# Part of the PSUM evictions moved from VectorE to ScalarE in a transformer layer on eight cores

## What is computed

```python
# attention part (input: layer-normed x)
xa = x @ (W_attn + lora).T                     # 3072 channels: q, k, v
xa = batchnorm(xa)                             # mean and variance over all 8*4096 rows
att = softmax(causal(q @ k.T / 32))
y = (att @ v) @ W_proj.T @ (W_proj + lora).T
x = x + layernorm(y)

# feed-forward part (input: layer-normed x)
aq(x) = round(x * 127 / max|x| per row), wq(w) = round(w / mean|w|) cut to -1..1
gate = silu(aq(x) @ wq(w_gate).T * scales)     # 1024 -> 4096
up   = aq(x) @ wq(w_up).T * scales             # 1024 -> 4096
down = aq(gate * up) @ wq(w_down).T * scales   # 4096 -> 1024
x = x + layernorm(down)
```

## Time and profile before

| | us |
|---|---|
| two timed runs | 6860.9 and 6988.77, median 6924.84 |
| profiled execution | 6855.12 |
| span of its slowest core (core 4) | 6853.6 |
| busy in it: PE, DVE, ACT, POOL | 4191.5, 2681.4, 859.0, 740.4 |
| stage 1b (1820 to 2211) | 391 |
| stage 4a (4665 to 5900) | 1235 |
| stage 4b (6008 to the end) | 846 |

### The profile page before, as it was taken

How to read it: one execution, slowest core, us unless ns; L and a number is a source line. 1 busy time by engine, 2 the same in 40 slices (tenths; PEclk the granted TensorE clock), 3 DMA queues, 4 the chain that set the end, 5 groups by cost and what they waited for, 6 DMA issues and landing times.

```text
span 6853.6 us, 63291 instructions; the slowest of 8 cores (6833.6 to 6853.6 us)
## 1 busy us (share of the span) xinstructions
PE 4191.5 (61%) x19100; PEld 1796.2 (26%) x19100; DVE 2681.4 (39%) x3728; ACT 859.0 (13%) x1490; POOL 740.4 (11%) x2436
## 2 busy tenths in 40 slices
PE   5455555799898124555556641116878787467676
PEld 2111111222443012222222221012333333233333
DVE  2444444300443233333333234445555555632322
ACT  0222222100000001111111111111111111000000
POOL 0244444300000000000000000000000000000000
PEclk9988888899999568788888885557989898688888
DMA  3766665565122211100000014441111111312221
GB/s 131 222 190 193 189 191 190 170 176 149 39 85 83 86 46 39 35 28 31 23 24 16 23 40 147 154 141 59 37 47 37 44 40 37 135 65 83 82 79 71
DMA packets 227896, 626.48 MB, mean 91 GB/s; under 512 B 56376, under 2 KB 81000, under 8 KB 215208
## 3 DMA queue, kind: packets, MB, share of 16 engines
q1 hardware_dynamic: 207080, 555.32, 25.9%
q0 software_dynamic: 20480, 67.13, 2.4%
HBM read 450.39 MB, written 171.97 MB: 91 GB/s over the span
## 4 chain that ended last, share of the span: by engine, by line
PE 48%; DVE 19%; issue 11%; DMA 10%; POOL 9%; ACT 1%; DVEq 1%; POOLq 1%; SPq 0%; ACTq 0%
PE pall L1322 8%; PE pall L1214 6%; PE pall L1207 6%; PE pall L680 5%; PE pall L930 4%; PE pall L532 4%; DVE lnx L491 3%; PE pall L827 2%; PE pall L845 2%; POOL lnx_scr L58 2%; POOL smalls L488 2%; PE pall L950 2%; PE pall L538 2%; PE pall L968 2%; DMA vbn<-xa_scr 1%
## 5 line engine op out<-in xcount | busy, mean ns | idle before, releaser
L508 PE MATMUL pall<-lnx 128*128 128x512 bf16 x2048 | 614.0, 453 | 456.0 <-DVE lnx L491 456.0
L1207 PE MATMUL pall<-WgT,kqT 128*128 128x512 bf16 x2048 | 536.5, 410 | 248.2 <-DVE kqT L1196 248.2
L1322 PE MATMUL pall<-WdT,gqT 128*128 128x512 bf16 x2048 | 516.1, 419 | 31.1 <-DVE gqT L1312 31.1
L1214 PE MATMUL pall<-WuT,kqT 128*128 128x512 bf16 x2048 | 500.8, 389 | 6.0 <-DVE gu L1226 5.9
L508 PEld LDWEIGHTS pall<-lnx 128*128 128x128 bf16 x2048 | 204.9, 108 | 864.8 <-issue 731.9
L491 DVE TENSOR_SCALAR lnx<-xin,smalls 128x1024 bf16<-128x1024 f32 x256 | 208.1, 813 | 565.3 <-POOL smalls L488 565.3
L827 PE MATMUL pall<-Kfm,qfm 128*128 128x512 bf16 (+3 forms) x480 | 167.9, 529 | 372.6 <-DVE smalls L896 341.9
L473 ACT ACTIVATE dummy1k<-xin 128x1024 f32<-128x1024 f32 x256 | 270.8, 1058 | 738.7 <-DMA xin<-x_all 738.2
L680 PE MATMUL pall<-lnfm,WqkvT 128*128 128x512 bf16 x1536 | 347.2, 390 | 6.2 <-DVE lnfm L662 6.2
L1207 PEld LDWEIGHTS pall<-WgT,kqT 128*128 128x128 bf16 x2048 | 208.8, 103 | 517.1 <-issue 305.7
L471 DVE TENSOR_REDUCE smalls<-xin 128x1 f32<-128x1024 f32 x256 | 310.6, 1213 | 5.6 <-DMA xin<-x_all 5.6
(11 more groups left out here) (216 smaller groups left out, 4912.4 us busy)
## 6 DMA issues: line engine op xcount, KB each, us to landing
xin<-x_all SPq DMA_DIRECT2D x256, 512.0 KB, 4.4
lnx_scr<-lnx POOLq DMA_DIRECT2D x256, 256.0 KB, 4.6
lnb<-lnx_scr SPq DMA_DIRECT2D x256, 256.0 KB, 2.7
wstg<-w_gate SPq DMA_DIRECT2D x64, 512.0 KB, 3.5
wstg<-w_up SPq DMA_DIRECT2D x64, 512.0 KB, 3.5
gq_scr<-gq SPq DMA_DIRECT2D x32, 1024.0 KB, 4.8
gq<-gq_scr SPq DMA_DIRECT2D x32, 1024.0 KB, 6.2
xa_scr<-stg SPq DMA_DIRECT2D x48, 512.0 KB, 2.9
```

Source lines behind the costliest of these rows:

```text
L508: s.add("pe", (lambda q, p=p, i=i, h=h, bi=bi, t=t: q.matmul(bank(bi), lnx[:, p, i * 128:(i + 1) * 128], lnx[:, p, h * 512:(h + 1) * 512], ...
L1207: s.add("pe", (lambda q, blk=blk, cj=cj, gb=gb, p=p: q.matmul(bank(gb), kqT[:, p, cj, :], WgT[:, cj, blk * 512:(blk + 1) * 512], start=(cj ...
L1214: s.add("pe", (lambda q, blk=blk, cj=cj, ub=ub, p=p: q.matmul(bank(ub), kqT[:, p, cj, :], WuT[:, cj, blk * 512:(blk + 1) * 512], start=(cj ...
L1322: s.add("pe", (lambda q, ds=ds, ic=ic, p=p: q.matmul(bank(ds), gqT[:, p, ic, :], WdT[:, ic, ds * 512:(ds + 1) * 512], start=(ic == 0), sto ...
```

## The change

Four groups of PSUM-to-SBUF copies move from VectorE (`tensor_copy`) to ScalarE (`copy`), some only in every second instance. Nothing else is changed: neither the order of the list, nor a buffer, nor a resource name.

- Stage 1b (L702): the odd ones of 24 copies per step, 96 of 192.
- V part (L794): the odd ones of 32.
- Stage 4a (L1196): all 32 copies to `kqT`.
- Stage 4b (L1312): lots 1 and 3 of each four, 64 of 128.

```diff
-                s.add("dve", (lambda q, djl=djl, bi=bi, sp_=sp_: q.tensor_copy(
-                    stg[:, sp_, djl, :], bank(bi))),
-                    reads=[PB[bi]], writes=[f"stg{sp_}"], name=f"eqkv{st}_{dj}")
+                eng_e = "dve" if dj % 2 == 0 else "act"
+                if eng_e == "dve":
...
+                else:
+                    s.add("act", (lambda q, djl=djl, bi=bi, sp_=sp_: q.copy(
+                        stg[:, sp_, djl, :], bank(bi))),
+                        reads=[PB[bi]], writes=[f"stg{sp_}"],
+                        name=f"eqkv{st}_{dj}")
...
+            if sk % 2 == 0:
...
+            else:
+                s.add("act", (lambda q, sp_=sp_, sk=sk, tb=tb: q.copy(
+                    Vtm[:, sp_ * 8 + sk, :], bank_bf(tb))),
+                    reads=[PB[tb]], writes=["Vtm"], name=f"evV{sp_}_{sk}")
...
-        s.add("dve", (lambda q, p=p: q.tensor_copy(
+        s.add("act", (lambda q, p=p: q.copy(
             kqT[:, p, :, :], bank_bf(6).rearrange("x (a b) -> x a b",
                                                   a=8, b=128))),
             reads=[PB[6]], writes=[f"kqT{p}"], name=f"ekq{t}")
...
+            if g4 % 2 == 0:
...
+            else:
+                s.add("act", (lambda q, g4=g4, tb=tb, p=p: q.copy(
+                    gqT[:, p, g4 * 8:(g4 + 1) * 8, :].rearrange(
+                        "x a b -> x (a b)"),
+                    bank_bf(tb))),
+                    reads=[PB[tb]], writes=[f"gqT{p}"], name=f"egq{t}_{g4}")
```

More of the change, by code:

```diff
@@ L701, in _build @@
                               reads=["dummy1k"], writes=["dbgdummy"], name="dbgl2")
-                s.add("dve", (lambda q, djl=djl, bi=bi, sp_=sp_: q.tensor_copy(
-                    stg[:, sp_, djl, :], bank(bi))),
-                    reads=[PB[bi]], writes=[f"stg{sp_}"], name=f"eqkv{st}_{dj}")
+                eng_e = "dve" if dj % 2 == 0 else "act"
+                if eng_e == "dve":
+                    s.add("dve", (lambda q, djl=djl, bi=bi, sp_=sp_:
+                                  q.tensor_copy(
+                        stg[:, sp_, djl, :], bank(bi))),
[3 more added lines that the diff above has]
+                    s.add("act", (lambda q, djl=djl, bi=bi, sp_=sp_: q.copy(
+                        stg[:, sp_, djl, :], bank(bi))),
+                        reads=[PB[bi]], writes=[f"stg{sp_}"],
+                        name=f"eqkv{st}_{dj}")
             if dbg and st == 0 and g == 0:
@@ L793, in _build @@
                     name=f"trV{sp_}_{sk}_{cj}")
-            s.add("dve", (lambda q, sp_=sp_, sk=sk, tb=tb: q.tensor_copy(
-                Vtm[:, sp_ * 8 + sk, :], bank_bf(tb))),
-                reads=[PB[tb]], writes=["Vtm"], name=f"evV{sp_}_{sk}")
+            if sk % 2 == 0:
+                s.add("dve", (lambda q, sp_=sp_, sk=sk, tb=tb: q.tensor_copy(
+                    Vtm[:, sp_ * 8 + sk, :], bank_bf(tb))),
+                    reads=[PB[tb]], writes=["Vtm"], name=f"evV{sp_}_{sk}")
+            else:
+                s.add("act", (lambda q, sp_=sp_, sk=sk, tb=tb: q.copy(
+                    Vtm[:, sp_ * 8 + sk, :], bank_bf(tb))),
+                    reads=[PB[tb]], writes=["Vtm"], name=f"evV{sp_}_{sk}")
     s.barrier("bar_P3")
@@ L1311, in transp4b @@
                     name=f"tgq{t}_{ic}")
[L1312 to L1316, removed]
+            if g4 % 2 == 0:
+                s.add("dve", (lambda q, g4=g4, tb=tb, p=p: q.tensor_copy(
+                    gqT[:, p, g4 * 8:(g4 + 1) * 8, :].rearrange(
[4 more added lines that the diff above has]
+                s.add("act", (lambda q, g4=g4, tb=tb, p=p: q.copy(
+                    gqT[:, p, g4 * 8:(g4 + 1) * 8, :].rearrange(
+                        "x a b -> x (a b)"),
+                    bank_bf(tb))),
+                    reads=[PB[tb]], writes=[f"gqT{p}"], name=f"egq{t}_{g4}")
     def mm4b(t):
```

## The result

| | before | after |
|---|---|---|
| median of the runs | 6857.8 us (6 runs) | 6945.0 us (7 runs) |
| profiled execution, its slowest core | 6853.6 us (core 4) | 6936.0 us (core 5) |
| stage 1b, first L680 to last | 385.0 | 382.5 |
| V part, first transpose to last | 123.9 | 121.7 |
| stage 4a, first gate group to last up group | 1227.6 | 1285.2 |

The changed kernel is slower by 1.26% (ratio 1.0126, 95% interval 1.0111 to 1.0141). In some executions of every kernel here the cores of one die, or of both, run at a lower clock and the whole takes 1 to 6% longer; ratios leave these executions out, and where too few others remain only the profiled execution and its stages are given. The profiled executions differ by 82.4 us, of which 4a has +57.6 and 4b +32.8; everything else together has -8.0.

A forecast was written before the change was run, and what follows sets the result against it. Stage 4a was taken as bound by a 38.36 us cycle over the xt load and chain4a, not the kqT wait. Terms +50 (4a), +23 (4b), +6 (V), -3 (1b) on 6855 give 6931 us, range 6862 to 7000.

The forecast's parts named there:

- The bound of 4a: Stage 4a: a 38.36 us cycle over the xt load and chain4a, without kqT, almost wholly covers the 7.8 us wait.
- The clock's term: Stage 4a: slow matmuls move onto the binding cycle, 2.25 us a tile; 4a +50 us, bounds -17 and +85.
- How the stall splits: Stage 4a: PE's stall of 7.9 us becomes two, 3.4 and 5.2 us, before block 3's gate and up groups.
- ScalarE's copy: Moved copies on ACT: 1.06 us taken for 128x1024, bounds 0.69 and 1.15, against 0.69 on DVE.
- rival 4: Stages 4a and 4b: copy not in ACT's loaded table, reloads of 1.283 us, +82 in 4b; 7014 us; chance 0.03.
- 4b: Stage 4b, between tiles: copies form one chain, the matmuls begin 0.7 us later; +23 us, bounds 0 and 38.
- V part and 1b: V copies wait for each other over Vtm, +6 us; in 1b an odd copy leaves DVE between steps, -3 us.
- The sum: Whole kernel: +50 + 23 + 6 - 3 = +76 us on 6855, giving 6931 us; chance 0.67.
- Rivals 1 and 2: Stage 4a: kqT wait was the bound, 6610 us, chance 0.06; clock doesn't fall or recovers early, 6864 us, chance 0.12.
- rival 3: Stage 4a: the clock costs more, 3.4 us a tile on the path, 4a +85; 6987 us; chance 0.12.

## Why the prediction was right, point by point

- **The bound of 4a.** Right. The cycle of 38.36 us was there as soon as the `kqT` wait was gone. With the clock held up the 30 tiles that have a `chain4a` averaged 38.47, and only moving the load and `chain4a` brought 33.25 and 29.48.
- **The clock's term.** Right in place, a little small in size. 2.25 us on top of 38.36 were foretold for each of 30 tiles, and 8.8 us off the last: +50. Measured are 40.88 us a tile, so 2.52 on top, and (38.64 - 29.5) = 9.1 off the last; 30 x (40.88 - 38.64) - 9.1 = +58, the stage's 57.6. The 2.25 was a mean over the slow stretches of before. The earlier trace rows show the clock only as far as 0.50; that it comes back to 1.00 stands in the windows above, from 5327.9 on. The run with filled pauses divides the 2.52: 40.88 - 38.47 = 2.41 are the clock, and 38.47 - 38.36 = 0.11 is the mean tile's length over the one tile that the cycle was read from. The upper bound of 3.4 us was put above half of the 6.0 us seen, and no run here comes near it.
- **How the stall splits.** Half right. I had one group at full speed between pauses of 3.4 and 5.2 us. The first pause already cost the clock in most tiles, so this group took 3.57 us and the second pause was 3.35: 111.8 us of waiting in place of 155. Pause, group and pause together come to the same 10.3 us, since L1240 ends the second pause at its own date.
- **ScalarE's copy.** 1.06 us was taken, 1.012 measured (128x1024), 0.586 for 128x512. "ScalarE: Activation LUTs" in the Trainium skill, section "What ACT_TABLE_LOAD costs", states a formula that gives an estimate of 1039 ns for this copy, closer than my row; the trace agrees within 3%. There are two table loads in the whole kernel, as before, and none in 4b, so rival 4 is out.
- **4b.** Right in mechanism, mis-sized. Foretold were +0.7 us a tile, all of it a later start; measured +0.98 (27.27 against 26.29). The tile of the earlier trace rows happened to be one with a late start of its own, 4.00 us behind the first copy. Most tiles before look like this one, with 3.65:

```profile
6035.07 0.68 DVE L1312 COPY gqT<-pall 128x1024 bf16<-128x1024 bf16 x1
...
6038.72 5.71 PE L1322 MATMUL pall<-WdT,gqT 128*128 128x512 bf16 x13 [0.95 <-DVE gqT L1312]
```

  After, it is 4.25 (6113.94 to 6118.19), so the start moved by 0.60. The rest is PE itself: its 2048 matmuls are busy for 529.7 us instead of 516.1, 0.42 us a tile, as more of them run at 0.50. The sum had no term for the clock in 4b, and that is the 10 us missing from it.
- **V part and 1b.** +6 and -3 were foretold. The table shows -2.2 and -2.5, but the -2.2 sets core 5 against core 4, whose 123.9 us is the longest V part of any core before (the others have 117.4 to 120.8). By the medians of eight cores the V part went from 119.6 to 122.4 us, +2.8, and 1b from 385.1 to 382.2, -2.9. So both signs were right, and the V part's term was about twice too large. What hides the rest of its slower copies was not tried.
- **The sum.** +76 us foretold, +82.4 between the profiled executions: 4a 8 and 4b 10 more, the rest of the kernel 11 less. That it comes so close is in part luck, since these misses cancel. Rivals 1 and 2 fell with the tile of 40.88 us, rival 3's 3.4 us a tile was not reached.

## What to carry to other kernels

A wait is worth its length only if no other cycle through the same stretch is as long. Before costing a cure, follow the chain of waits over one whole period and look for a period that doesn't contain the wait; if it is within a few per cent, cure both or neither. And moving work to a second engine costs time while both write one resource name: +1.0 us a tile in the old order of 4b, +1.7 in the new one. Split the name first, and then see whether the second engine is needed at all. In 4b the split was worth 2.1 us a tile with VectorE alone, and ScalarE added nothing to it; in 4a, where the copy stood behind VectorE's two long passes, ScalarE was worth 8.4.

## What the hardware showed that I had not expected

- TensorE's clock was lost without one long pause. With no pause over 1.41 us but three in a row, it fell (0.50 for 3.3 us a tile); in another kernel it fell behind 23 of 30 single pauses of 2.36 to 2.74 us. "TensorE: Matmul & The Clock Gate" in the Trainium skill, section "What's actually happening", ties the clock to recent activity, and the traces agree that idle time is what brings it down. But no length of a pause tells the two cases apart here: it held behind seven single pauses of 2.36 to 2.38 us, and with filled pauses ahead it held in some tiles through 1.16, 0.55 and 1.41 us in a row.
- Where a slow stretch falls matters more than whether there is one. The 6 us at 0.50 of the earlier trace rows lay beside another chain, and the mean tile was only 38.64 - 38.36 = 0.3 us over that chain's length; the slow stretch on the binding cycle cost 40.51 - 38.18 = 2.3 us a tile.
